# Turning the normal rows of six tiles by transposing transfers instead of TensorE, with the gates and deltas one tile later

## The chip, the cores and the metric

The kernel runs on one core of a Trainium2 chip. The metric is device time in microseconds of one execution; lower is better. An execution has five engines: TensorE (PE in the profile, its weight loads PEld), VectorE (DVE), ScalarE (ACT), GpSimd (POOL) and SyncE (SP), which here only issues transfers.

## The reference

Two residual steps on `x` of shape 2 x 1024 x 2048 (16 tiles of 128 rows):

```python
def _L0_xattn_ref(x1, x2, ...):            # fake_quant: round to 8-bit codes, and back
    return jnp.matmul(fake_quant(x1, ...), fake_quant(x2, ...))

def _L0_ffn_ref(x, A, B, Wr):              # 4 experts of rank 16, the best 2 per row
    logits = flat @ Wr.T
    gates = softmax(logits where it is one of the top 2, else -inf)
    mid = jnp.einsum('tf,erf->ter', flat, A)
    all_deltas = jnp.einsum('ter,eor->teo', mid, B) * SCALE
    return jnp.sum(gates[:, :, None] * all_deltas, axis=1)

x = x + jnp.tanh(g_xattn[0]) * _L0_xattn_ref(_layernorm(x), ctx_4096, ...)
x = x + jnp.tanh(g_ffn[0]) * _L0_ffn_ref(_layernorm(x), A, B, Wr)
```

## The kernel before, in words

Raw Bass, one program per engine, each written out in order and held together by semaphores. `ctx` is kept in SBUF as 8-bit codes in fp16 (`q2`), 16 blocks of 128 rows by 2048 columns per batch. Rows of x go through these steps, tile by tile, with five slots of `xr` (RING) in a ring:

- **codes**: `stats_x`, `var_x`, `scale_of_x` on VectorE (with `power_x` on GpSimd between), `scale_x` on ScalarE makes the byte codes, `turn_q1` on TensorE turns them into PSUM (`ps_gate`), `copy_q1T` on ScalarE brings them to `q1T`. `sum_codes` and `shift_of_row` carry a correction for the second batch.
- **product**: `main(b, n)` on TensorE, 16 matmuls for each of four column blocks n, into two banks `ps_main` in turn. `add_main(b, n)` on VectorE adds the result to `xr`; main(b, n) waits until the add two blocks before is done.
- **normal rows**: `stats_h` per block, `var_h`, `power_h` (GpSimd), `bias_h`; then `high_part` on ScalarE writes the fp16 high part `h_hi` of all 2048 columns, `normal_half` writes the fp32 value for each half, and `low_part` on GpSimd subtracts and writes the fp16 rest `h_lo`.
- **turning them**: `turn_hi(b, h)` on TensorE turns one half (8 blocks of 128x128) of `h_hi` into the PSUM bank `ps_turn[h]`, and `copy_hiT` on ScalarE brings it to `hT`; then `turn_lo` turns the low half into the same bank, and `copy_loT` (half 0 on ScalarE, half 1 on VectorE) brings it to the same `hT`, once `mid_hi` has used the high part.
- **small product**: `mid_hi` and `mid_lo` multiply the turned halves by `a_parts` (A and Wr) into `ps_mid`. `rank_gates` and `weigh` on VectorE (with `gate_exp` on ScalarE between) make the weighted middle values `gated`; `turn_gate` turns these into `ps_gate`, `split_gate` copies them to `gT_hi` and `gT_lo`, and `delta(b, n)` multiplies by B, two matmuls per block, into `ps_delta`. `add_delta` adds to `xr`, and `store` writes the tile out.

The order of all this is fixed by hand. Up to tile 8 (counting from 0) every call stands alone; from STEADY = 9 on a loop over b makes the order of each tile, and this is the part that the change rewrites. In one turn of it TensorE multiplies tile b, turns and multiplies the normal rows of tile b-1, makes the deltas of tile b-2, and turns the codes of tile b+1:

```python
for b in range(STEADY, TILES):
    main(b, 0, general, 0, 4)
    delta(b - 2, 0)
    delta(b - 2, 1)
    ...
    main(b, 2, general, 10)
    if b < LAST:
        turn_q1(b + 1, b - 1)
    mid_lo(b - 1, 0)
    mid_lo(b - 1, 1)
    main(b, 3, general, 0, 14)
    turn_gate(b - 1, min(b + 2, TILES))
    main(b, 3, general, 14)
```

After the loop comes a tail for tile 15 alone, which is not changed but for the counts of its waits. SP issues all transfers in one order of its own: in each turn the two stores of tile b-2, then, once these have landed, the two loads of tile b+3.

## Time and profile before

| | us |
|---|---|
| median of 3 runs (lowest to highest) | 359.08 (357.84 to 359.25) |
| the profiled execution's own time | 358.96 |
| its span, first to last instruction | 357.1 |
| busy in the span: TensorE, VectorE, ScalarE, GpSimd | 331.5, 280.4, 268.9, 109.4 |
| mean granted TensorE clock | 0.998 of full |

A busy share is a mean over stages with different limits. The windows view gives the busy time of each engine in a stretch; the chain of waits follows the work that ended last back from the last instruction; the timeline lists instructions in order of their start, each with its duration and what ended the idle time before it. A matmul's end is modelled, and it overlaps the next one, so its duration there (0.38 us for 512 columns) is longer than its share in the chain.

### The profile page before, as it was taken

How to read it: one execution, taken by the hardware profiler on the slowest of the kernel's cores; microseconds unless marked ns; L12 is line 12 of the kernel's file. 1: busy time of each engine (PE TensorE's matmuls, PEld its weight loads, DVE VectorE, ACT ScalarE, POOL GpSimd, SP SyncE). 2: the span in 40 equal slices, each digit the busy share in tenths (PEclk: the TensorE clock that was granted, in tenths of full speed). 3: DMA queues.
4: the chain of work that ended last, by engine and by line, in shares of the span. 5: the costliest groups of instructions: out<-in, count | busy, mean ns of one | idle time of the engine just before them, and what ended most of it. 6: DMA issues, size and time to landing. Idle time of an engine off the chain costs nothing.

```text
span 357.1 us, 6514 instructions
## 1 busy us (share of the span) xinstructions
PE 331.5 (93%) x2372; PEld 186.5 (52%) x2372; DVE 280.4 (79%) x701; ACT 268.9 (75%) x239; POOL 109.4 (31%) x123
## 2 busy tenths in 40 slices
PE   0489999999999999999999999999999999999984
PEld 0134544456665465545566565655656464656552
DVE  5798679978879778974888968779696969784785
ACT  1699799999999989898995566667858666666150
POOL 3100333245647161333432050505042240505000
PEclk9999999999999999999999999999999999999999
DMA  7999999904299759796024940423323111102023
GB/s 216 415 419 422 418 419 417 422 37 129 108 317 392 208 196 295 284 338 215 13 106 169 300 147 35 162 75 123 118 102 135 59 61 60 61 0 119 0 111 127
DMA packets 19185, 69.17 MB, mean 194 GB/s; under 512 B 2256, under 2 KB 2256, under 8 KB 19024
## 3 DMA queue, kind: packets, MB, share of 16 engines
q1 hardware_dynamic: 19152, 68.73, 51.6%
q8 instruction: 21, 0.34, 0.4%
q14 instruction: 12, 0.10, 0.1%
HBM read 51.94 MB, written 16.78 MB: 192 GB/s over the span
## 4 chain that ended last, share of the span: by engine, by line
PE 72%; DMA 11%; DVE 7%; issue 3%; ACT 3%; SPq 2%; POOL 1%; DVEq 0%; ACTq 0%; POOLq 0%
PE ps_main L741 40%; DMA xr<-in_x 6%; DMA out_x<-xr 5%; PE ps_delta L741 4%; PE ps_mid L797 4%; PE ps_turn L785 3%; PE ps_turn L778 3%; PE ps_turn L741 3%; PE ps_delta L824 3%; PE ps_delta L826 3%; PE ps_gate L741 2%; PE ps_mid L741 2%; PE ps_mid L805 2%; DVE small_tile L1236 1%; DVE xr L1292 1%
## 5 line engine op out<-in xcount | busy, mean ns | idle before, releaser
L741 PE MATMUL ps_main<-q,q1T 128*128 128x512 f16 x832 | 201.3, 379 | 1.5 <-DVE xr L1292 0.8
L741 PEld LDWEIGHTS ps_main<-q,q1T 128*128 128x128 f16 x832 | 76.8, 98 | 84.2 <-issue 8.7
L414 POOL TENSOR_TENSOR h_parts<-work,h_parts 128x512 f16<-128x512 f32 x30 | 34.2, 1160 | 53.4 <-ACT work L547 53.4
L541 ACT ACTIVATE h_parts<-xr,small_tile 128x2048 f16<-128x2048 f32 x15 | 31.4, 2092 | 24.6 <-DVE small_tile L1309 23.2
L1236 DVE BATCH_NORM_STATS2 small_tile<-xr 128x6 f32<-128x512 f32 x64 | 40.8, 682 | 7.4 <-DMA xr<-in_x 7.3
L1292 DVE SCALAR_TENSOR_TENSOR xr<-ps_main,small_tile,xr 128x512 f32<-128x512 f32 x52 | 38.6, 743 | 9.3 <-PE ps_main L741 9.3
L507 ACT ACTIVATE c_code<-q,small_tile 128x1024 uint8<-128x1024 f32 x32 | 37.8, 1236 | 9.5 <-DMA q<-in_ctx 8.3
L1297 DVE BATCH_NORM_STATS2 small_tile<-xr 128x6 f32<-128x512 f32 x64 | 43.7, 688 | 0.8
L553 ACT COPY hT<-ps_turn 128x1024 f16<-128x1024 f16 x32 | 31.4, 1006 | 13.4 <-PE ps_turn L778 13.3
L405 POOL TENSOR_TENSOR small_tile<-small_tile 128x1 f32<-128x1 f32 x16 | 8.8, 549 | 99.6 <-DVE small_tile L1305 99.6
L514 ACT ACTIVATE x_byte<-xr,small_tile 128x2048 uint8<-128x2048 f32 x16 | 33.4, 2090 | 6.6 <-DVE small_tile L1251 6.6
L414 POOL TENSOR_TENSOR h_parts<-q1T,h_parts 128x512 f16<-128x512 f32 x30 | 34.2, 1161 | 2.1 <-ACT q1T L547 2.1
L824 PE MATMUL ps_delta<-lora_bT,gT_hi 128*128 128x512 f32 x60 | 30.5, 508 | 0.2
L531 ACT ACTIVATE q1T<-ps_gate,small_tile 128x2048 f16<-128x2048 uint8 x12 | 23.5, 1961 | 2.3 <-PE ps_gate L724 2.3
L712 PE MATMUL ps_main<-ident_h 128*128 128x512 f16 x47 | 13.3, 432 | 12.5 <-issue 12.5
L400 POOL TENSOR_TENSOR small_tile<-small_tile 128x1 f32<-128x1 f32 x16 | 9.3, 584 | 49.9 <-DVE small_tile L1243 49.9
L1315 DVE COPY hT<-ps_turn 128x1024 f16<-128x1024 f16 x16 | 11.0, 689 | 17.2 <-PE ps_turn L785 17.0
L507 ACT ACTIVATE q<-q,small_tile 128x1024 uint8<-128x1024 f32 x20 | 24.3, 1236 | 0.2
L826 PE MATMUL ps_delta<-lora_bT,gT_lo 128*128 128x512 f32 x60 | 23.8, 396 | 0.0
L1366 DVE TENSOR_TENSOR xr<-ps_delta,xr 128x512 f32<-128x512 f32 x32 | 21.5, 682 | 1.0 <-PE ps_delta L826 0.8
L1223 DVE TENSOR_SCALAR q<-c_code,small_tile 128x1024 f16<-128x1024 f16 x32 | 18.9, 597 | 4.2 <-ACT c_code L507 4.0
L1369 DVE SCALAR_TENSOR_TENSOR xr<-ps_delta,small_tile,xr 128x512 f32<-128x512 f32 x30 | 21.6, 743 | 0.8 <-PE ps_delta L837 0.6
(132 smaller groups left out, 501.3 us busy)
## 6 DMA issues: line engine op xcount, KB each, us to landing
q<-in_ctx SPq DMA_DIRECT2D x52, 512.0 KB, 14.9
xr<-in_x SPq DMA_DIRECT2D x32, 512.0 KB, 6.2
out_x<-xr SPq DMA_DIRECT2D x30, 512.0 KB, 3.7
c_code<-in_ctx SPq DMA_DIRECT2D x6, 512.0 KB, 5.9
q1T<-in_ctx SPq DMA_DIRECT2D x6, 512.0 KB, 6.3
h_parts<-in_B SPq DMA_DIRECT2D x1, 1024.0 KB, 17.6
out_x<-xr SPq DMA_DIRECT2D x4, 256.0 KB, 2.2
xr<-in_A SPq DMA_DIRECT2D x1, 544.0 KB, 16.5
```

Of the source, the lines that this page charges most:

```text
L414: nc.gpsimd.tensor_tensor(h_lo[:, half(h)][:, part], work[h][:, part], h_hi[:, half(h)][:, part], ALU.subtract).then_inc(h_lo_ready, 1)
L507: nc.scalar.activation(byte, stage(i), ACT.Identity, bias=par[:, 3:4], scale=inv_s[:, 1:2]).then_inc(row_scaled, 1)
L514: nc.scalar.activation(x_byte[:, :], xr[:, b % RING, :], ACT.Identity, bias=q_scale[:, 1:2], scale=q_scale[:, 0:1]).then_inc(x_scaled, 1)
L531: nc.scalar.activation(q1T_of(b).rearrange("p (j two) m -> p j two m", two=2), as16(turn_bank(b), U8).rearrange("p (j m two) -> p j two m" ...
L541: nc.scalar.activation(h_hi[:, :], xr[:, b % RING, :], ACT.Identity, bias=h_bias[:, b % 2:b % 2 + 1], scale=h_rstd[:, b % 2:b % 2 + 1]).th ...
L553: nc.scalar.copy(hT[:, h, :, :], as16(ps_turn[h], F16).rearrange("p (k m) -> p k m", m=P)).then_inc(hiT_ready, 1)
L741: mm = pe.matmul(product_bank(b, n)[:, :], q1T_of(b)[:, k, :], q2[:, batch(b), slot(batch(b), k), cols(n)], start=(k == 0), stop=(k == KT ...
L824: pe.matmul(ps_delta[n % 2][:, :], gT_hi[:, :], lora_bT[:, cols(n)], start=True, stop=False)
L826: pe.matmul(ps_delta[n % 2][:, :], gT_lo[:, :], lora_bT[:, cols(n)], start=False, stop=True).then_inc(delta_done, 1)
L1236: nc.vector.bn_stats(x_stats[:, n, :], xr[:, b % RING, cols(n)]).then_inc(x_stats_done, 1)
L1292: nc.vector.scalar_tensor_tensor(out=x1, in0=product_bank(b, n)[:, :], scalar=gain[:, 0:1], in1=x1, op0=ALU.mult, op1=ALU.add).then_inc(x1 ...
L1297: nc.vector.bn_stats(h_stats[:, b % 2, n, :], xr[:, b % RING, cols(n)]).then_inc(h_stats_done, 1)
```

## The change

For the tiles in MOVED (8 to 13 counted from 0, which the words of the change count as 9 to 14) the eight blocks of each half are turned by a transposing transfer from SBUF to SBUF on SP's queue: `move_hi` from `h_hi` to `hT`, and `move_lo` from `h_lo` to a buffer of its own, `loT`, which lies on the fourth plane of `q1T`. The four turns on TensorE and the four copies (three on ScalarE, one on VectorE) are not made for these tiles. `mid_hi` and `mid_lo` wait for the transfers instead, `high_part` and `low_part` wait until the transfer of the tile before has read the old values, and `mid_hi` and `mid_lo` stand later among the products.

The counts of the other waits on `hi_turned`, `hiT_ready`, `lo_turned` and `loT_ready` go by `turned(b)`, the number of tiles before b that TensorE turns. The core of the diff, with the indentation cut by eight:

```diff
+MOVED = range(STEADY - 1, 14)
...
+def turned(b):
+    return len([t for t in range(b) if t not in MOVED])
+def moved(b):
+    return len([t for t in range(b) if t in MOVED])
...
+loT = q1T[:, 3, :, :].rearrange("p (h k) m -> p h k m", h=2)
...
+    def move_hi(b, h):
+        sp.wait_ge(h_hi_ready, b + 1)
+        sp.wait_ge(hi_used, 2 * (b - 1) + h + 1)
+        sp.wait_ge(lo_used, 2 * turned(b))
+        sp.dma_start_transpose(hT[:, h, :, :], h_hi[:, half(h)]).then_inc(hi_moved[h], 16)
+
+    def move_lo(b, h):
+        sp.wait_ge(h_lo_ready, 4 * b + 2 * h + 2)
+        sp.wait_ge(row_scaled, 4 * KT)
+        sp.wait_ge(lo_used, 2 * (b - 1) + h + 1)
+        sp.dma_start_transpose(loT[:, h, :, :], h_lo[:, half(h)]).then_inc(lo_moved[h], 16)
...
     for b in range(STEADY, TILES):
-        for h in range(2):
-            store(b - 2, h)
+        if b - 1 in MOVED:
+            move_hi(b - 1, 0)
+            move_hi(b - 1, 1)
+            move_lo(b - 1, 0)
+            store(b - 2, 0)
+            move_lo(b - 1, 1)
+            store(b - 2, 1)
+        else:
+            for h in range(2):
+                store(b - 2, h)
         if b + 3 < TILES:
             load_x(b + 3, 0)
             load_x(b + 3, 1)
...
         pool.wait_ge(h_hi_ready, b + 1)
-        wait(pool, lo_turned, 2 * (b - 1) + h + 1)
+        if b - 1 in MOVED:
+            pool.wait_ge(lo_moved[h], 16 * moved(b))
+        else:
...
     for b in range(STEADY, TILES):
         power_h(b - 1)
         low_part(b - 1, 0)
-        low_part(b - 1, 1)
         if b < LAST:
             power_x(b + 1)
+        low_part(b - 1, 1)
     power_h(LAST)


...
-        wait(act, hi_turned, 2 * b)
+        if b - 1 in MOVED:
+            for h in range(2):
+                act.wait_ge(hi_moved[h], 16 * moved(b))
+        else:
+            wait(act, hi_turned, 2 * turned(b))
...
     for b in range(STEADY, TILES):
+        if b > STEADY:
+            gate_exp(b - 2)
         high_part(b - 1)
         normal_half(b - 1, 0)
         normal_half(b - 1, 1)
-        copy_hiT(b - 1, 0)
-        copy_hiT(b - 1, 1)
+        if b - 1 not in MOVED:
+            copy_hiT(b - 1, 0)
+            copy_hiT(b - 1, 1)
         if b < LAST:
             scale_x(b + 1)
-        copy_loT(b - 1)
+        if b - 1 not in MOVED:
+            copy_loT(b - 1)
         if b < LAST:
             copy_q1T(b + 1)
-        gate_exp(b - 1)
-        if b < LAST:
             sum_codes(b + 1)
+        else:
+            gate_exp(b - 1)

     act.wait_ge(h_bias_ready, TILES)
-    act.wait_ge(hi_turned, 2 * LAST)
+    act.wait_ge(hi_turned, 2 * turned(LAST))
     act.wait_ge(h_lo_ready, 4 * LAST)
     for h in range(2):
         nc.scalar.activation(h_hi[:, half(h)], xr[:, LAST % RING, half(h)], ACT.Identity,
...
     def mid_lo(b, h):
-        pe.wait_ge(loT_ready[h], b + 1)
+        if b in MOVED:
+            pe.wait_ge(lo_moved[h], 16 * moved(b + 1))
+        else:
+            pe.wait_ge(loT_ready[h], turned(b) + 1)
         for k in range(HK):
             kk = h * HK + k
-            mm = pe.matmul(ps_mid[:, J:2 * J], hT[:, h, k, :], a_parts[:, kk, 0, :], start=False, stop=(kk == KT - 1))
+            mm = pe.matmul(ps_mid[:, J:2 * J], (loT if b in MOVED else hT)[:, h, k, :], a_parts[:, kk, 0, :], start=False, stop=(kk == KT - 1))
         mm.then_inc(lo_used, 1)
     def turn_gate(b, q1):
...
         turn_gate(7, 10)
         main(8, 3, general, 13, 16)
         for b in range(STEADY, TILES):
-            main(b, 0, general, 0, 4)
-            delta(b - 2, 0)
-            delta(b - 2, 1)
-            main(b, 0, general, 4)
+            main(b, 0, general)
+            if b == STEADY:
+                delta(b - 2, 0)
+                delta(b - 2, 1)
+            main(b, 1, general, 0, 6)
+            if b > STEADY:
+                turn_gate(b - 2, b + 1)
+            main(b, 1, general, 6, 12)
+            if b > STEADY:
+                delta(b - 2, 0)
+                delta(b - 2, 1)
+            main(b, 1, general, 12)
+            if b - 1 not in MOVED:
+                turn_hi(b - 1, 0)
+                turn_hi(b - 1, 1)
+            main(b, 2, general, 0, 10)
             delta(b - 2, 2)
             delta(b - 2, 3)
-            main(b, 1, general)
-            turn_hi(b - 1, 0)
-            turn_hi(b - 1, 1)
-            main(b, 2, general, 0, 10)
+            main(b, 2, general, 10, 12)
             mid_hi(b - 1, 0)
-            turn_lo(b - 1, 0)
+            if b - 1 not in MOVED:
+                turn_lo(b - 1, 0)
+            main(b, 2, general, 12)
             mid_hi(b - 1, 1)
-            turn_lo(b - 1, 1)
-            main(b, 2, general, 10)
+            if b - 1 not in MOVED:
+                turn_lo(b - 1, 1)
+            main(b, 3, general, 0, 2)
             if b < LAST:
                 turn_q1(b + 1, b - 1)
-            mid_lo(b - 1, 0)
-            mid_lo(b - 1, 1)
-            main(b, 3, general, 0, 14)
-            turn_gate(b - 1, min(b + 2, TILES))
+            main(b, 3, general, 2, 6)
+            if b - 1 not in MOVED:
+                mid_lo(b - 1, 0)
+                mid_lo(b - 1, 1)
+            main(b, 3, general, 6, 14)
+            if b - 1 in MOVED:
+                mid_lo(b - 1, 0)
+                mid_lo(b - 1, 1)
             main(b, 3, general, 14)
+            if b - 1 not in MOVED:
+                turn_gate(b - 1, TILES)
         delta(LAST - 1, 0)
         delta(LAST - 1, 1)
         pe.wait_ge(x1_ready, NB * LAST + 3)
...
     stats_h(8, 2)
     for b in range(STEADY, TILES):
-        split_gate(b - 2)
+        if b > STEADY:
+            rank_gates(b - 2)
+        else:
+            split_gate(b - 2)
         add_main(b - 1, 3)
         stats_h(b - 1, 3)
         var_h(b - 1)
-        add_delta(b - 2, 0)
+        if b > STEADY:
+            weigh(b - 2)
         bias_h(b - 1)
-        add_delta(b - 2, 1)
         if b < LAST:
             stats_x(b + 1, 0)
         add_main(b, 0)
+        if b > STEADY:
+            split_gate(b - 2)
+        else:
+            add_delta(b - 2, 0)
         shift_of_row(b)
         stats_h(b, 0)
-        add_delta(b - 2, 2)
-        add_delta(b - 2, 3)
         if b < LAST:
             stats_x(b + 1, 1)
             var_x(b + 1)
+        if b > STEADY:
+            add_delta(b - 2, 0)
+        add_delta(b - 2, 1)
         add_main(b, 1)
-        stats_h(b, 1)
         if b < LAST:
             scale_of_x(b + 1)
-        copy_loT(b - 1)
+        add_delta(b - 2, 2)
+        add_delta(b - 2, 3)
+        stats_h(b, 1)
+        if b - 1 not in MOVED:
+            copy_loT(b - 1)
         add_main(b, 2)
-        rank_gates(b - 1)
+        if b == LAST:
+            rank_gates(b - 1)
         stats_h(b, 2)
-        weigh(b - 1)
+        if b == LAST:
+            weigh(b - 1)
     split_gate(LAST - 1)
     add_main(LAST, 3)
     stats_h(LAST, 3)
```

Three places show what it moves. On TensorE, the small product of tile 13 and around it, in the time of tile 14 (L741 and L785 are the products, L797 and L844 `mid_hi`, L805 and L855 `mid_lo`; `h_parts` is `h_hi` and `h_lo`, `q1T` beside `a_parts` is `loT`). Before:

```order
L778 MATMUL ps_turn0<-ident_h,h_parts 128x128 x8
L778 MATMUL ps_turn1<-ident_h,h_parts 128x128 x8
L741 MATMUL ps_main0<-q2,q1T 128x512 x10
L797 MATMUL ps_mid<-a_parts,hT 128x136 x8
L785 MATMUL ps_turn0<-ident_h,h_parts 128x128 x8
L797 MATMUL ps_mid<-a_parts,hT 128x136 x8
L785 MATMUL ps_turn1<-ident_h,h_parts 128x128 x8
L741 MATMUL ps_main0<-q2,q1T 128x512 x6
L724 MATMUL ps_gate<-ident_h,x_byte 128x128 x8
L805 MATMUL ps_mid<-a_parts,hT 128x68 x16
L741 MATMUL ps_main1<-q2,q1T 128x512 x14
L816 MATMUL ps_gate<-ident_f,gated 128x128
```

Now:

```order
L785 MATMUL ps_main0<-q2,q1T 128x512 x2
L844 MATMUL ps_mid<-a_parts,hT 128x136 x8
L785 MATMUL ps_main0<-q2,q1T 128x512 x4
L844 MATMUL ps_mid<-a_parts,hT 128x136 x8
L785 MATMUL ps_main1<-q2,q1T 128x512 x2
L768 MATMUL ps_gate<-ident_h,x_byte 128x128 x8
L785 MATMUL ps_main1<-q2,q1T 128x512 x12
L855 MATMUL ps_mid<-a_parts,q1T 128x68 x16
L785 MATMUL ps_main1<-q2,q1T 128x512 x2
```

The four turns are gone; `mid_hi` of half 0 stands 12 products into block 2, and `mid_lo` two products ahead of the end of block 3, where it stood ahead of block 3.

On VectorE, the start of tile 15's time. Before (L1357 and L1359 are `split_gate`, L1292 `add_main`, L1369 `add_delta`):

```order
L1357 CAST gT_hi<-ps_gate 128x128
L1359 TENSOR_TENSOR gT_lo<-ps_gate,gT_hi 128x128
L1292 SCALAR_TENSOR_TENSOR xr<-ps_main1,small_tile,xr 128x512
L1297 BN_STATS small_tile<-xr 128x6
L1302 BN_AGGR small_tile<-small_tile 128x2
L1305 TENSOR_SCALAR small_tile<-small_tile 128x1
L1369 SCALAR_TENSOR_TENSOR xr<-ps_delta0,small_tile,xr 128x512
L1309 TENSOR_SCALAR small_tile<-small_tile 128x1
L1369 SCALAR_TENSOR_TENSOR xr<-ps_delta1,small_tile,xr 128x512
```

Now (the ranking of tile 13 stands ahead of the first row; L1360 is `add_main`, L1409 to L1417 are `weigh`, L1377 is `bias_h`, L1425 and L1427 are `split_gate`):

```order
L1360 SCALAR_TENSOR_TENSOR xr<-ps_main1,small_tile,xr 128x512
L1365 BN_STATS small_tile<-xr 128x6
L1370 BN_AGGR small_tile<-small_tile 128x2
L1373 TENSOR_SCALAR small_tile<-small_tile 128x1
L1409 SCALAR_TENSOR_TENSOR ps_mid<-ps_mid,small_tile 128x64
L1413 TENSOR_REDUCE small_tile<-ps_mid 128x1
L1415 RECIPROCAL small_tile<-small_tile 128x1
L1417 SCALAR_TENSOR_TENSOR gated<-mids,small_tile,ps_mid 128x128
L1377 TENSOR_SCALAR small_tile<-small_tile 128x1
L1360 SCALAR_TENSOR_TENSOR xr<-ps_main0,small_tile,xr 128x512
L1425 CAST gT_hi<-ps_gate 128x128
L1427 TENSOR_TENSOR gT_lo<-ps_gate,gT_hi 128x128
```

Ranking and weighing of tile b-2, at the end of tile b-1's time before, now stand around `var_h` of tile b-1, and `split_gate` behind the first block of tile b.

On SP, the stores and loads from tile 10's loads on. Before:

```order
L269 DMA xr<-in_x 128x1024 x4
L290 DMA out_x<-xr 128x1024 x2
L269 DMA xr<-in_x 128x1024 x2
L290 DMA out_x<-xr 128x1024 x2
L269 DMA xr<-in_x 128x1024 x2
```

Now:

```order
L282 DMA xr<-in_x 128x1024 x4
L309 DMA_TRANSPOSE hT<-h_parts 128x8x128 x2
L315 DMA_TRANSPOSE q1T<-h_parts 128x8x128
L303 DMA out_x<-xr 128x1024
L315 DMA_TRANSPOSE q1T<-h_parts 128x8x128
L303 DMA out_x<-xr 128x1024
L282 DMA xr<-in_x 128x1024 x2
```

Four transposing transfers stand in each turn, two ahead of the stores' place and two among them.

## Rows read from the trace of the kernel before

**Rows 1.** The page's part 1, busy us, share of the span and instructions.
```profile
PE 331.5 (93%) x2372; PEld 186.5 (52%) x2372; DVE 280.4 (79%) x701; ACT 268.9 (75%) x239; POOL 109.4 (31%) x123
```

**Rows 2.** Windows: length, then busy us of each engine, clock, DMA share, GB/s.
```profile
core 0: us, PE busy (x) PEld busy (x) DVE busy (x) ACT busy (x) POOL busy (x), PEclk, DMA share, GB/s
200.80:339.00 138.20, 137.78 (x1008) 78.96 (x1007) 106.61 (x280) 89.32 (x85) 38.44 (x41) 1.00 0.25 93
240.25:260.00 19.75, 19.71 (x147) 11.34 (x145) 15.74 (x42) 13.62 (x13) 5.56 (x6) 1.00 0.31 109
```

**Rows 3.** Chain of waits, time of tile 11: start us, us, what.
```profile
238.04 1.29 PE ps_main L741 x6
239.34 0.23 PE ps_delta L824
...
247.26 0.89 PE ps_turn L778 x16
...
250.31 0.47 PE ps_mid L797 x8
250.78 0.45 PE ps_turn L785 x8
...
253.89 0.50 PE ps_mid L805 x16
...
257.45 0.33 PE ps_gate L816
257.78 1.29 PE ps_main L741 x6
```

**Rows 4.** Timeline, tile 11's time: start, us, engine, line, operation, tiles, idle before.
```profile
242.14 1.28 DVE L1236 BATCH_NORM_STATS2 small_tile<-xr 128x6 f32<-128x512 f32 x2
...
243.33 0.73 DVE L1292 SCALAR_TENSOR_TENSOR xr<-ps_main,small_tile,xr 128x512 f32<-128x512 f32 x1
...
244.90 2.28 POOL L414 TENSOR_TENSOR h_parts<-work,h_parts 128x512 f16<-128x512 f32 x2 [3.59 <-ACT work L547]
...
254.43 0.31 DVE L1322 TENSOR_REDUCE ps_mid<-ps_mid 128x68 f32<-128x136 f32 x1 [0.19 <-PE ps_mid L805]
...
255.80 0.68 DVE L1297 BATCH_NORM_STATS2 small_tile<-xr 128x6 f32<-128x512 f32 x1
...
256.40 0.22 DVE L1341 SCALAR_TENSOR_TENSOR ps_mid<-ps_mid,small_tile 128x64 f32<-128x64 f32 x1
...
257.04 0.35 DVE L1349 SCALAR_TENSOR_TENSOR gated<-mids,small_tile,ps_mid 128x128 f32<-128x128 f32 x1
...
258.35 0.74 DVE L1292 SCALAR_TENSOR_TENSOR xr<-ps_main,small_tile,xr 128x512 f32<-128x512 f32 x1
...
260.34 0.75 DVE L1369 SCALAR_TENSOR_TENSOR xr<-ps_delta,small_tile,xr 128x512 f32<-128x512 f32 x1
...
261.33 2.09 ACT L541 ACTIVATE h_parts<-xr,small_tile 128x2048 f16<-128x2048 f32 x1 [3.03 <-DVE small_tile L1309]
```

**Rows 5.** Timeline, the end of tile 15's products.
```profile
332.30 0.66 PE L805 MATMUL ps_mid<-a_parts,hT 128*128 128x68 f16 x16
...
333.17 0.30 DVE L1322 TENSOR_REDUCE ps_mid<-ps_mid 128x68 f32<-128x136 f32 x1
...
336.55 0.29 DVE L1357 CAST gT_hi<-ps_gate 128x128 fp32r<-128x128 f32 x1 [0.42 <-PE ps_gate L816]
...
336.89 0.50 PE L824 MATMUL ps_delta<-lora_bT,gT_hi 128*128 128x512 f32 x1
337.08 0.74 DVE L1292 SCALAR_TENSOR_TENSOR xr<-ps_main,small_tile,xr 128x512 f32<-128x512 f32 x1
```

**Rows 6.** The page's parts 3 and 6: the queue, and stores to landing.
```profile
q1 hardware_dynamic: 19152, 68.73, 51.6%
...
out_x<-xr SPq DMA_DIRECT2D x30, 512.0 KB, 3.7
...
out_x<-xr SPq DMA_DIRECT2D x4, 256.0 KB, 2.2
```

19 lines of the change are left out of this document (12 added, 7 removed).

## The prediction

> **What bounds the kernel now.** I read the page's busy shares first: TensorE is busy for 93% of the span, VectorE for 79%, ScalarE for 75% [rows 1]. A mean over stages says little, so the windows come next. In the steady part, 200.8 to 339 us, TensorE is busy 137.78 of 138.20 us at full granted clock, and in the window of one tile (240.25 to 260.00) it is busy 19.71 of 19.75 us, against 15.74 for VectorE and 13.62 for ScalarE [rows 2]. There TensorE alone sets the time, and what leaves its stream is gained until some other chain is late. The chain of waits, third, shows what one tile's 19.74 us (238.04 to 257.78) is made of: products at 1.29 us for six, 0.215 each; 0.89 us for the 16 transposes of the high part; 0.45 us for each 8 of the low part, twice; 0.47 us for each half of the high product; 0.50 us for the low product; 0.33 us for the gate's turn; 0.23 us for each of 8 delta matmuls [rows 3].
>
> **The change part by part.** *Transposes off TensorE.* Each of six tiles (9 to 14 in the title's count, indices 8 to 13 in the code, turned in the time of tiles 9 to 14) loses 0.89 + 2 x 0.45 = 1.79 us of transposes [rows 3]. All of it lies on the path: 6 x 1.79 = **-10.74 us**. One transpose costs 0.056 us there, since they run in a stream. The Trainium skill, VectorE: DVE Perf Modes, section The three transpose paths, has 390 ns for a 128x128 turn on TensorE; by an estimate from that page the 192 would be worth 75 us. The trace disagrees with 56 ns, and the measurement decides. ScalarE loses three copies a tile and VectorE one; neither bounds, so they count as nothing. If TensorE stopped bounding they would matter, and VectorE, at 15.74 us less one copy against a new period of about 18.0, has only some 3 us of slack.
>
> *Gates and deltas moved.* rank_gates, weigh and split_gate of tile b-2 now run in tile b, ahead of or between the steps that make tile b-1's normal rows. The question is whether the new order keeps pace. I lay it out from the start of rank_gates(b-2) as 0, with the intervals of the old order [rows 4]. Ranking takes 1.37 us (254.43 to 255.80). add_main, stats_h and var_h take 1.99 (258.35 to 260.34), so weigh starts at 3.36; it reaches its last operation after 0.64 and ends at 4.35. bias_h follows at about 4.3, h_hi's activation 0.25 later, and it ends after 2.09 us at 6.6. stats_x starts at 4.4, add_main(b, 0) 1.19 later at 5.6, the cast to gT_hi about 0.65 after that (0.73 us less the overlap), and it ends at 6.53. On TensorE, the low product that released rank_gates ended 0.04 us before 0. Then come 24 products (5.18), the gate's turn (0.33; its operand has been there since 4.4) and six products (1.29), so the first delta matmul should end at about 7.0. In the last tile, where a delta found its weights not yet loaded, it ended 0.55 us after the cast did (336.84 to 337.39) [rows 5]: here 7.08. The two weights together make me put **+0.2 us** on each of five tiles, **+1.0 us** in all, with 0 and 0.4 a tile as ends. The same delay covers turn_q1, whose codes come at 14.35 by this reckoning, just when TensorE wants them. delta(b-2, 2) and (b-2, 3) want their banks at 10.7 and 11.2 and VectorE frees them at 10.3 and 10.9: no wait, but little room.
>
> *The last tile.* There tile 14 is still turned by TensorE, but mid_lo(14) stands six products later than before: 6 x 0.215 = **+1.30 us**. Everything after it hangs on VectorE: rank_gates started at 333.17 and the last add_main at 337.08, 3.91 us later, with the same operations between them as in the new order [rows 5]. So TensorE's products, which now end 2.16 us after mid_lo, no longer cover that chain, and the engine idles for about a microsecond ahead of the gate's turn. What comes back is that rank_gates, which waited 0.21 us past mid_lo's end (332.96) for VectorE [rows 5], will wait 0.04: **-0.17 us**.
>
> *The four transfers a tile.* SP issues each one when its source half is ready. The high halves come at 6.65 and are wanted at 12.1 and 13.4 (12 and 16 products into the third column block). GpSimd starts the first low half at 7.85 and needs 2.28 us for it [rows 4], so it goes out at 10.2 and is wanted at 17.4; the second, after power_x, goes out at 13.0 and is wanted at 17.6. The queue also carries the stores, and the second load_x of an iteration waits for them; those loads are out by about 17 and SP is next wanted at 24.6, so SP blocks nothing. No row shows a transposing transfer. From below, a store of the same 256 KB landed in 2.2 us, of which 0.7 is the bytes at the queue's mean rate while busy (68.73 MB in 51.6% of 357.1 us, 0.373 MB/us) and 1.5 is fixed [rows 6]. From above: the queue's 19152 packets took 51.6% of 16 engines' 357.1 us, 154 ns each [rows 6]. If each 256-byte run of a row costs as much as such a packet, a half is 1024 runs, 64 an engine, 9.9 us, and 11.4 with the fixed part. Call the queue time of a half D, between 0.7 and 9.9. Nothing is late while 8.15 + 2D stays under 13.4 and 8.15 + 4D + 1.3 (a store between) under 17.6, which is D up to 2.0. I take D = 1.5, near the lower end: it is what the stores pay for 256 KB more (3.7 against 2.2) [rows 6], the nearest row by bytes, and double the mean rate's price. So the transfers cost nothing, hidden behind the 5 to 7 us of products ahead of each use.
>
> Sum: -10.74 + 1.0 + 1.30 - 0.17 = -8.6 us. The profiled execution took 358.96 us (span 357.1); that gives 350.3. It stands 0.12 us under the median of 359.08, so no further shift.
>
> **The rivals.** *Transposing transfers are slow (slower than before).* If the price goes by short runs, the queue runs without a pause from 6.65 on and mid_lo waits for the fourth half: each tile is late by 9.45 + 4D - 17.6. The 8.6 us are used up at 1.4 us a tile, D = 2.4; past that the kernel is slower. At D = 4, the geometric middle between my value and the upper end, a tile is 7.85 us late, the total 358.96 - 8.6 + 6 x 7.85 = 397 us; at 9.9 it would be about 540. For it: four small-run transfers a tile in series, and the one bound that rows give from above. Against it: the queue is busy for 25% of the steady part [rows 2], and the bytes are few. I give it 18%. The same section of the Trainium skill speaks against this change: it has 1309 ns for a 128x128 turn by transfer and advises TensorE where a PSUM destination will do; eight blocks in series would be 10.5 us a half by an estimate from it, this rival at its upper end. No row here shows it.
>
> *A new VectorE chain takes most of it.* The margins above are 0.1 to 0.4 us and rest on some 25 intervals. If the chain to gT_hi, or to add_delta, runs 0.5 to 1 us longer, TensorE waits that much in each of five tiles: 352.8 to 355.3. Together with transfers a little late (D 2.0 to 2.3) I give it 14%. For it: VectorE has waits of its own between nearly all of these small operations. Against it: the intervals come from the same operations in the same form.
>
> *No gain to be seen*, where D is close to 2.4, or the tail loses several us more than I have: 358 or 359 us, 8%. That the transfers are not made, or made late because SP stands at another wait, I hold to be out: they stand in SP's order, and no wait ahead of them ends after 17 us of the previous tile's time.
>
> **How the numbers follow.** Forecast as above 60%, its own range 348.3 to 352.5 (0 to 0.4 us of wait a tile, and 1 us for the tail). To take in the second case and the third the range goes up to 360.9; 18% lie above, nearly nothing below. A measurement of this kernel can tell some 0.5%, 1.8 us, from no change: faster by more 0.74, within it 0.08, slower by more 0.18.
>
> **What the new profile would show.** Right: a tile's period of 18.0 to 18.3 us in the chain of waits; 192 fewer transposes on TensorE; no wait for hT or q1T ahead of the products of a_parts; transfers landing 3 to 5 us after issue; about 0.2 us at the delta behind the cast to gT_hi; 1 us idle before the last turn of a gate. Wrong: a TensorE wait released by a DMA in each tile (the slow transfers), or by gT_hi, x_byte or out_ready for over 0.4 us a tile (the VectorE chain); or a granted clock under 1 in the tail from the added idle time.

## The result, and the profile after

| | before | after |
|---|---|---|
| median of 4 runs each, us | 358.92 (357.84 to 359.25) | 349.29 (349.14 to 350.64) |
| ratio, 95% interval | | 0.9744 (0.9722 to 0.9765) |
| profiled execution, us (span) | 358.96 (357.1) | 350.64 (348.9) |
| period of a steady tile, us | 19.76 | 18.12 |
| from the seventh index's gate cast to the last one, us | 152.13 | 143.10 |

The changed kernel is 2.6% faster; 350.3 us had been predicted. Medians here and in the table of experiments are over executions in the fast state; the two slower ones, 393.37 us in experiment 2 and 352.95 us in experiment 4, are left out. The last row of the table needs a word. Executions of one kernel reach the steady part at different times: the cast to gT_hi of tile index 7, the last one that no experiment here touches, stands at 198.36 us in the profile before and at 199.14 after, and over all runs below between 196.9 and 199.6. From there on a tile's period repeats to 0.02 us in most kernels. So small effects are read from that cast to the last cast of the program. These are VectorE's timeline rows of the kernel before:

```profile
198.36 0.29 DVE L1357 CAST gT_hi<-ps_gate 128x128 fp32r<-128x128 f32 x1 [0.30 <-PE ps_gate L816]
...
350.49 0.29 DVE L1357 CAST gT_hi<-ps_gate 128x128 fp32r<-128x128 f32 x1 [0.42 <-PE ps_gate L816]
```

and the same two of the kernel after:

```profile
199.14 0.29 DVE L1425 CAST gT_hi<-ps_gate 128x128 fp32r<-128x128 f32 x1 [0.29 <-PE ps_gate L866]
...
342.24 0.29 DVE L1425 CAST gT_hi<-ps_gate 128x128 fp32r<-128x128 f32 x1 [0.42 <-PE ps_gate L866]
```

By this measure the change brought 152.13 - 143.10 = 9.03 us. The page of the kernel after, its parts 1 and 3:

```profile
PE 321.4 (92%) x2180; PEld 175.4 (50%) x2180; DVE 276.0 (79%) x695; ACT 252.2 (72%) x221; POOL 109.5 (31%) x123
...
DMA packets 44528, 75.45 MB, mean 216 GB/s; under 512 B 27600, under 2 KB 27600, under 8 KB 44368
...
q1 hardware_dynamic: 44496, 75.02, 63.3%
```

TensorE has the 192 matmul instructions less that the order of work had promised [rows 1]. The queue carries 25344 packets more than before [rows 6], 1056 for each of the 24 transposing transfers, and is busy for 0.633 x 348.9 - 0.516 x 357.1 = 36.6 us more, 1.52 us a half. The next answer is the stretch of one tile, from one first delta to the next, in the windows view:

```profile
core 0: us, PE busy (x) PEld busy (x) DVE busy (x) ACT busy (x) POOL busy (x), PEclk, DMA share, GB/s
...
241.67:259.80 18.13, 18.07 (x113) 9.44 (x114) 14.70 (x41) 10.80 (x12) 5.58 (x6) 1.00 0.68 175
```

TensorE still looks busy for 18.07 of 18.13 us, at full granted clock, as before [rows 2]. The share of busy time hides what the chain of waits shows:

```profile
240.77 0.65 DVE xr L1360
241.42 0.21 DVE gT_hi L1425
241.67 0.50 PE ps_delta L874
...
252.66 0.51 PE ps_mid L855 x16
253.20 0.32 DVE ps_mid L1390
...
258.90 0.65 DVE xr L1360
259.55 0.21 DVE gT_hi L1425
259.80 0.50 PE ps_delta L874
```

Before, the chain stayed on TensorE for the whole tile [rows 3]. Now the turns (L778 and L785 of the kernel before) are gone, and in each tile the chain leaves TensorE at the low product (253.20), runs for 6.6 us through VectorE (ranks, the fourth add_main, statistics, weigh, add_main(b, 0)) to gT_hi and comes back with the first delta. That is a closed loop at the pace of the tile. The waits of the stretch from 200 to 320 us name it, and the room that VectorE has left elsewhere:

```profile
DVE ps_mid L1390 <- PE ps_mid L855: 16.2, 6, 3.0
...
PEld ps_delta L874 <- DVE gT_hi L1425: 2.7, 5, 0.6
PEld ps_gate L768 <- ACT x_byte L550: 1.5, 5, 0.3
```

TensorE's weight load waits for gT_hi in five tiles, while VectorE stood idle 2.7 us ahead of ranking, for the low product. The weight load of the codes' turn waits too, 0.3 us a tile, but the turn itself starts no later behind its products than in experiment 1 below (0.43 us from the first of its two products to it, 249.03 to 249.46). No wait is released by a transfer. The four transfers of this tile in SP's timeline:

```profile
241.73 2.59 SPq L309 DMA_TRANSPOSE hT<-h_parts  x2
245.22 1.23 SPq L315 DMA_TRANSPOSE q1T<-h_parts  x1
246.51 1.42 SPq L303 DMA_DIRECT2D out_x<-xr  x1
248.03 1.60 SPq L315 DMA_TRANSPOSE q1T<-h_parts  x1
249.68 0.57 SPq L303 DMA_DIRECT2D out_x<-xr  x1
252.93 0.81 SPq L282 DMA_DIRECT2D xr<-in_x  x2
```

With the start of ranking at 235.07 (253.20 less a period), the reckoning of the prediction has them at 241.72, 245.27 and 248.07. The time to landing is in the two lines' own answers, first L309, then L315:

```profile
DMA to landing us min/median/max: 2.7/2.7/2.8
DMA to landing us min/median/max: 2.7/2.7/4.4
```

The medians hide something. The second low half, the last of the four, landed after 2.7 us in the first two moved tiles, but after 3.6, 4.4, 4.4 and 4.2 us in the other four. TensorE wants it when the second half of the low product starts, 0.25 us into that product. In the tile of 266.12 us it landed at 270.52 and was wanted at 270.88: the room was 0.36 us (landings are given to 0.1 us), and 1.1 us in the tile shown.

At the end of tile 15, TensorE's timeline shows the idle time that the late low product of tile index 14 leaves [rows 5 for before]:

```profile
324.20 0.66 PE L855 MATMUL ps_mid<-a_parts,hT 128*128 128x68 f16 x16
...
327.92 0.33 PE L866 MATMUL ps_gate<-ident_f,gated 128*128 128x128 f32 x1 [0.90 <-DVE gated L1417]
328.63 0.50 PE L874 MATMUL ps_delta<-lora_bT,gT_hi 128*128 128x512 f32 x1 [0.38 <-DVE gT_hi L1425]
```

### The profile page after: what moved, and what is told of

It is laid out like the page before. It is cut to its first block, busy times and chain, and to the rows that moved or that the text cites. A ratio compares the mean times of both kernels' runs of the same rounds, so it can differ in the third digit from the quotient of the medians.

```text
span 348.9 us, 6112 instructions
## 1 busy us (share of the span) xinstructions
PE 321.4 (92%) x2180; PEld 175.4 (50%) x2180; DVE 276.0 (79%) x695; ACT 252.2 (72%) x221; POOL 109.5 (31%) x123
## 4 chain that ended last, share of the span: by engine, by line
PE 62%; DVE 14%; DMA 12%; issue 4%; ACT 3%; SPq 3%; POOL 1%; DVEq 0%; ACTq 0%; POOLq 0%
PE ps_main L785 32%; DMA out_x<-xr 5%; DMA xr<-in_x 4%; PE ps_delta L785 4%; PE ps_mid L844 4%; DMA q<-in_ctx 4%; PE ps_delta L874 3%; PE ps_turn L785 3%; PE ps_delta L876 3%; DVE xr L1360 3%; DVE small_tile L1304 2%; PE ps_mid L785 2%; PE ps_gate L785 2%; PE ps_mid L855 2%; PE ps_turn L829 2%
## 5 line engine op out<-in xcount | busy, mean ns | idle before, releaser
L785 PE MATMUL ps_main<-q,q1T 128*128 128x512 f16 x832 | 201.9, 379 | 2.8 <-DVE xr L1360 2.0
L785 PEld LDWEIGHTS ps_main<-q,q1T 128*128 128x128 f16 x832 | 76.1, 98 | 84.4 <-issue 8.6
L1360 DVE SCALAR_TENSOR_TENSOR xr<-ps_main,small_tile,xr 128x512 f32<-128x512 f32 x52 | 38.5, 741 | 3.4 <-PE ps_main L785 3.4
L1291 DVE TENSOR_SCALAR q<-c_code,small_tile 128x1024 f16<-128x1024 f16 x32 | 20.5, 647 | 3.7 <-ACT c_code L543 3.5
L844 PEld LDWEIGHTS ps_mid<-a_parts,hT 128*128 128x128 f16 x256 | 17.3, 98 | 7.1 <-issue 1.0
L456 POOL MEMSET q<- 128x1024 f32 x16 | 15.1, 955 | 18.1 <-ACT q L543 9.3
```

The source lines that it names most:

```text
L785: mm = pe.matmul(product_bank(b, n)[:, :], q1T_of(b)[:, k, :], q2[:, batch(b), slot(batch(b), k), cols(n)], start=(k == 0), stop=(k == KT ...
L844: mm = pe.matmul(ps_mid[:, 0:2 * J], hT[:, h, k, :], a_parts[:, kk, :, :].rearrange("p c j -> p (c j)"), start=(kk == 0), stop=False)
L1360: nc.vector.scalar_tensor_tensor(out=x1, in0=product_bank(b, n)[:, :], scalar=gain[:, 0:1], in1=x1, op0=ALU.mult, op1=ALU.add).then_inc(x1 ...
```

## The experiments

Eleven kernels were run. All but the seventh start from the kernel after; tile numbers in them are the program's indices, so the six moved tiles are 8 to 13 and the last is 15. "Cast to cast" is the measure of the section above; differences between kernels are by it unless a clock time is named. Each ratio is to executions of the kernel before that were taken beside it, with medians of 358.73 us for experiments 1 to 4, 359.24 for 5 to 8 and 359.63 for 9 to 11, so it is not the quotient of two rows of the table.

| kernel | median, us | ratio to before, 95% | cast to cast, us | period, us |
|---|---|---|---|---|
| before | 358.92 | | 152.13 | 19.76 |
| after | 349.29 | 0.9744 (0.9722 to 0.9765) | 143.10 | 18.12 |
| 1 order only | 358.69 | 1.0001 (0.9987 to 1.0015) | 151.80 | 19.50 |
| 2 three tiles | 354.04 | 0.9856 (0.9827 to 0.9886) | 147.65 | 18.12, then 19.5 |
| 3 tile 14 too | 348.92 | 0.9719 (0.9696 to 0.9742) | 141.82 | 18.12 |
| 4 tile 14, deltas later | 347.22 | 0.9700 (0.9673 to 0.9728) | 141.61 | 18.08 |
| 5 low product sooner | 348.48 | 0.9703 (0.9682 to 0.9724) | 141.25 | 17.70 to 17.87 |
| 6 much sooner | 348.30 | 0.9705 (0.9664 to 0.9746) | 141.21 | 17.72 to 17.84 |
| 7 before, gate later | 359.89 | 1.0019 (1.0002 to 1.0036) | 152.47 | 19.87 |
| 8 last tile as before | 349.19 | 0.9736 (0.9704 to 0.9769) | 141.96 | 18.12 |
| 9 transfers only | 355.99 | 0.9902 (0.9875 to 0.9928) | 149.09 | 19.23 |
| 10 low halves twice | 355.98 | 0.9905 (0.9877 to 0.9933) | 149.52 | 18.9 to 19.7 |
| 11 tile 14 and sooner | 346.39 | 0.9622 (0.9599 to 0.9645) | 139.39 | 17.70 to 17.79 |

### 1. The order alone

```diff
-MOVED = range(STEADY - 1, 14)
+MOVED = range(STEADY - 1, STEADY - 1)
...
-                    if b - 1 not in MOVED:
+                    if b == LAST:
                         turn_gate(b - 1, TILES)
```

> The changed kernel's order of work with no tile moved: TensorE turns both parts of every tile, 192 transposes more than in the changed kernel, while gates, deltas and low products stay a tile later than before. My theory (the gain is the 192 transposes, and the new order costs about 1.3 us at the end): 359 to 361 us, a period of 19.7 to 20.0 us per tile in the steady part, ratio to the kernel before 1.000 to 1.006. Rival (the gain comes from the new order, which takes waits off TensorE): 350 to 355 us. A second rival (the new order costs more than the sum had, and the transposes brought more than 10.7 us): above 361 us.

Measured: 358.69 us, ratio 1.0001, no difference by the clock; 151.80 us cast to cast, 0.33 less than before. So on top of the new order the transfers bring 151.80 - 143.10 = 8.70 us; what they bring without it is experiment 9. But the period was not what I had expected. TensorE's timeline of this kernel:

```profile
242.51 0.27 PE L866 MATMUL ps_gate<-ident_f,gated 128*128 128x128 f32 x1
...
243.72 0.58 PE L874 MATMUL ps_delta<-lora_bT,gT_hi 128*128 128x512 f32 x1
...
262.01 0.27 PE L866 MATMUL ps_gate<-ident_f,gated 128*128 128x128 f32 x1
```

Gate to gate is 19.50 us, 0.26 under the kernel before. This order therefore has a floor for the changed kernel: 19.51 - 1.79 = 17.72 us, not the 17.97 that one gets from the period before. And from the gate's turn to the first delta, with the same six products between, this kernel takes 243.72 - 242.51 = 1.21 us. The kernel after takes 1.62:

```profile
258.18 0.27 PE L866 MATMUL ps_gate<-ident_f,gated 128*128 128x128 f32 x1
258.29 1.46 PE L785 MATMUL ps_main<-q,q1T 128*128 128x512 f16 x6
259.80 0.50 PE L874 MATMUL ps_delta<-lora_bT,gT_hi 128*128 128x512 f32 x1
```

The wait for gT_hi thus costs 0.41 us a tile, twice what the sum had, and the new order gave back 0.25 a tile that the sum did not have.

### 2. Three tiles instead of six

```diff
-MOVED = range(STEADY - 1, 14)
+MOVED = range(STEADY - 1, 11)
...
```

The condition of the last turn_gate is changed as in experiment 1.

> Only tiles 8 to 10 of the program's count (three of six) are turned by transfers; tiles 11 to 13 go through TensorE in the new order. My theory (each moved tile gains by itself, 1.79 us of transposes less about 0.2 us of new wait): 349.3 + 3 x 1.6 = 354.1 us, between 353.6 and 355.0. Rival (the gain is one step, had once from the order): within 1 us of 349.3 or of 359. In the trace: tiles 8 to 10 at a period of 18.1 us, tiles 11 to 13 at 19.7 to 20.0.

Measured: 354.04 us, 147.65 cast to cast. The first three moved tiles bring 151.80 - 147.65 = 4.15 us, the next three 4.55. Both come out of the two numbers of experiment 1: three tiles' transposes at 1.79 us, less 0.41 us for each wait at gT_hi. Three such waits are in this kernel's timeline (1.62 us from gate to first delta, then 1.21), and two more in the kernel after, since tile 15 has none: 5.37 - 1.23 = 4.14 and 5.37 - 0.82 = 4.55. The gain is had tile by tile; the rival of one step falls.

### 3. Tile 14 by transfer as well

```diff
-MOVED = range(STEADY - 1, 14)
+MOVED = range(STEADY - 1, 15)
...
-                    if b - 1 not in MOVED:
+                    if b == LAST:
                         mid_lo(b - 1, 0)
                         mid_lo(b - 1, 1)
...
```

The waits of the tail on the turns of tile 14 become waits on its landings. mid_lo(14) stays behind six products of the fourth block, where the kernel after has it; the expectation has it four products later, which is not what the edit does.

> Tile 14 of the program's count is turned by transfers as well, so that only the last tile's normal rows go through TensorE. 32 more transposes leave TensorE (1.79 us), and mid_lo(14) comes another four products later, behind the landing of the second low half. My theory (TensorE sets the period, transfers are hidden): 349.3 - 1.8 + 0.2 = 347.7 us, between 347.3 and 348.3. Rival 1 (the tail is bound by VectorE's ranks and add_mains after mid_lo, so that a later mid_lo costs as much as the transposes give): 349.3 us or more, up to 350.5. Rival 2 (transfers collide with the last loads and stores): a wait of TensorE on a landing in tile 15.

Measured: 348.92 us by the clock, hardly a difference; 141.82 cast to cast, 1.28 less than after, where 1.6 was expected. Rival 2 is there in a small way: this is the first transfer that TensorE waits for, since mid_lo stands early in this tile. TensorE's timeline:

```profile
322.69 0.41 PE L856 MATMUL ps_mid<-a_parts,q1T 128*128 128x68 f16 x8
323.45 0.42 PE L856 MATMUL ps_mid<-a_parts,q1T 128*128 128x68 f16 x8 [0.34 <-DMA q1T<-h_parts]
...
326.93 0.33 PE L867 MATMUL ps_gate<-ident_f,gated 128*128 128x128 f32 x1 [0.90 <-DVE gated L1418]
```

The second half of the low product starts 0.76 us behind the first instead of 0.25, so the landing costs 0.51 us, and 1.79 - 0.51 is the 1.28 measured. The 0.90 us ahead of the gate's turn is as it was: VectorE's chain behind the low product still sets the end.

### 4. Tile 14, with deltas and codes two products later

The edit of experiment 3, and besides:

```diff
-                    main(b, 1, general, 6, 12)
+                    main(b, 1, general, 6, 14)
                     if b > STEADY:
                         delta(b - 2, 0)
                         delta(b - 2, 1)
-                    main(b, 1, general, 12)
+                    main(b, 1, general, 14)
...
-                    main(b, 3, general, 0, 2)
+                    main(b, 3, general, 0, 4)
                     if b < LAST:
                         turn_q1(b + 1, b - 1)
-                    main(b, 3, general, 2, 6)
+                    main(b, 3, general, 4, 6)
```

> As the run with tile 14 too, and besides in every steady tile both halves of the delta come two products later in TensorE's order (behind 14 products instead of 12), and the turn of the next tile's codes two products later as well. My theory (VectorE's rank chain ends 0.16 us per tile after TensorE wants the first delta, and the codes come in step with it, so both have to move): 347.7 - 6 x 0.15 = 346.8 us, between 346.4 and 347.3, period 17.97 to 18.0. Rival (the wait merely moves on, because VectorE's next add_main or rank comes later by as much, a closed loop): within 0.3 us of the run with tile 14 too.

Measured: a period of 18.08 us and 141.61 cast to cast, 0.21 less than the run before it. The rival was right. The wait for gT_hi is gone (1.65 us from gate to first delta, with eight products between), but the next one stands behind it, at the second pair of deltas. TensorE's timeline here, from the first of the twelve products ahead of that pair:

```profile
240.86 1.47 PE L786 MATMUL ps_main<-q,q1T 128*128 128x512 f16 x6
...
243.56 0.47 PE L875 MATMUL ps_delta<-lora_bT,gT_hi 128*128 128x512 f32 x1
...
244.22 0.47 PE L875 MATMUL ps_delta<-lora_bT,gT_hi 128*128 128x512 f32 x1
```

and in the kernel after, with fourteen products ahead of it:

```profile
242.80 1.47 PE L785 MATMUL ps_main<-q,q1T 128*128 128x512 f16 x6
...
245.65 0.58 PE L874 MATMUL ps_delta<-lora_bT,gT_hi 128*128 128x512 f32 x1
```

The pair comes 2.70 us behind the first product here and 2.85 there. Two products less are 0.43 us less, so it starts 0.28 us late; it then takes 1.21 us instead of 1.13. Together that is 0.36 us, all that the period lies above 17.72. The view of waits names no releaser for it (eight waits of the weight load, 3.1 us in four tiles), but the two add_delta that free the banks are in VectorE's timeline from 242.67 to 244.08, and the second delta starts 0.14 us behind the end of the second:

```profile
242.67 1.41 DVE L1438 SCALAR_TENSOR_TENSOR xr<-ps_delta,small_tile,xr 128x512 f32<-128x512 f32 x2
```

Moving the consumer back doesn't help in a closed loop; the start of VectorE's chain has to come sooner. By the clock this kernel looks 1.7 us better than the third. In the two profiled executions, 347.19 and 349.62 us, the difference is 2.43 us, and 2.22 of it stands at the cast of tile index 7 (197.20 against 199.42 us), ahead of anything that the two do differently. That is the spread of the start, not the edit.

### 5. The low product two products sooner

```diff
-                    main(b, 3, general, 6, 14)
+                    main(b, 3, general, 6, 12)
                     if b - 1 in MOVED:
                         mid_lo(b - 1, 0)
                         mid_lo(b - 1, 1)
-                    main(b, 3, general, 14)
+                    main(b, 3, general, 12)
```

> The changed kernel with mid_lo(b-1) two products sooner (behind 12 products of the fourth block instead of 14) in the five steady tiles. VectorE stood idle 2.7 us a tile for this product, and its chain from there to gT_hi set TensorE's wait of 0.41 us a tile (18.12 us against 19.51 - 1.79 = 17.72 by the run of the order alone). My theory now: the chain starts 0.43 us sooner, the wait is gone, a period of 17.70 to 17.80 us, 5 x 0.4 = 2.0 us less from the first moved tile's cast to the last cast than the changed kernel's 143.10: 141.1; by the clock some 347.3 us, with the 1 us by which executions of one kernel differ before the steady part. Rival 1 (the wait is set by something else than VectorE's start, its own length or the ring of buffers): 18.08 to 18.12. Rival 2 (the second low half lands too late for the sooner product): a TensorE wait released by the transfer into q1T, and a period between the two.

Measured: 141.25 us cast to cast (141.1 expected), ratio 0.9703. From gate to first delta TensorE now takes 1.22 us, as in the first experiment:

```profile
256.12 0.27 PE L866 MATMUL ps_gate<-ident_f,gated 128*128 128x128 f32 x1
...
257.34 0.58 PE L874 MATMUL ps_delta<-lora_bT,gT_hi 128*128 128x512 f32 x1
```

The period is 17.70 us in three of five tiles, 17.78 and 17.87 in two. This shows both the floor of 17.72 and the cause of the 0.41 us: the loop started late by two products, while VectorE stood idle ahead of it.

The two longer tiles are the transfer's, as far as the times tell. In them the low product, 0.66 us long in the other tiles, lasts 0.73 and 0.83 us:

```profile
249.94 0.73 PE L855 MATMUL ps_mid<-a_parts,q1T 128*128 128x68 f16 x16
```

The other stands at 285.43. There the second low half was handed out at 281.33 and landed 4.5 us later, at 285.83, where its product wanted it at 285.68; in the tile shown it landed at 250.21 and was wanted at 250.19. In the tiles of 17.70 us it landed in time. The view of waits lists nothing as short as 0.07 or 0.17 us, so this rival 2, small, is read from the times and not named by the profile.

### 6. Four products sooner

The same edit with 10 in the place of 12.

> mid_lo(b-1) four products sooner (behind 10 products). In the changed kernel the second low half is handed out at 248.03 us and takes up to 4.0 us to land, 252.0; this order wants it at 251.6 less 0.4 for the shorter period. My theory (transfers were hidden with 0.5 to 1 us to spare and no more): TensorE waits 0.2 to 0.9 us a tile for the transfer, so that the period is 17.9 to 18.6 us, worse than with two products sooner. Rival (the margin is large, transfers are never late): no wait on a transfer, a period of 17.72.

Measured: a period of 17.72 us in three tiles, 17.74 and 17.84 in the last two, and no wait on a transfer in the view of waits; the rival was right about the period. But the margin is small. The second low half landed after 2.7 us in the first two tiles and after 3.7 to 4.4 us in the last four, about as long as I had taken it for. What I had wrong is when it is handed out: the sooner low product starts VectorE's next chain sooner too, so that the half goes out at 246.38 us, 1.93 us ahead of the codes' turn, where the kernel after has 1.43. The second half of the low product wants it at 250.74, 4.36 us later. In the last tile it landed at 303.96 and was wanted at 303.92, and that low product lasts 0.78 us instead of 0.66: the 0.12 us of the 17.84. Four products are not better than two, since TensorE is at its floor with either, and later than here the transfer must not land.

### 7. The kernel before, with the gate's turn later

```diff
-                    main(b, 0, general, 0, 4)
+                    main(b, 0, general, 0, 6 if b > STEADY else 4)
                     delta(b - 2, 0)
                     delta(b - 2, 1)
-                    main(b, 0, general, 4)
+                    main(b, 0, general, 6 if b > STEADY else 4)
...
-                    main(b, 3, general, 0, 14)
+                    main(b, 3, general)
                     turn_gate(b - 1, min(b + 2, TILES))
-                    main(b, 3, general, 14)
```

> The kernel before, with the turn of the gate two products later (behind the whole fourth block) and, so as to keep the distance, the first two deltas two products later too, in the steady part. My theory (the kernel before lost 0.25 us a tile because TensorE stood at the gate's turn until VectorE had written gated; the sum took that loss for work): a period of 19.50 to 19.55 us against 19.76, 6 x 0.22 = 1.3 us less, 357.4 us, ratio 0.996. Rival (the 0.25 us that the order alone brought comes from the other moves): a period of 19.74 to 19.78, no change.

Measured: 359.89 us, ratio 1.0019 (1.0002 to 1.0036), a period of 19.87 us in the profile, longer by 0.11 us a tile; a ratio of 1.0019 is at the edge of what the medians tell. Neither theory had that. The gate's turn now takes its plain 0.11 us, but the low product waits instead, for ScalarE's copy of the turned low half, in TensorE's timeline:

```profile
254.53 0.67 PE L805 MATMUL ps_mid<-a_parts,hT 128*128 128x68 f16 x16 [0.21 <-ACT hT L558]
```

In the kernel before, it was the weight load of the gate's turn that waited, in its waits of the same stretch:

```profile
PEld ps_gate L816 <- DVE gated L1349: 1.6, 3, 0.5
```

So the 0.25 us of the kernel before was also the loss of a loop, and two products more at one place move it. Which of the moves in the new order breaks that loop (the copies, the statistics of x, the deltas) is not told apart by these runs; that the whole of them does is shown by the first.

### 8. The last tile in its old order

```diff
...
+                    if b == LAST:
+                        mid_hi(b - 1, 0)
+                        turn_lo(b - 1, 0)
+                        mid_hi(b - 1, 1)
+                        turn_lo(b - 1, 1)
+                        main(b, 2, general, 10)
+                        mid_lo(b - 1, 0)
+                        mid_lo(b - 1, 1)
+                        main(b, 3, general, 0, 14)
...
```

The other tiles keep the order of the kernel after.

> The changed kernel with mid_hi(14), turn_lo(14) and mid_lo(14) of the last tile back at their places in the kernel before, six products sooner for mid_lo. My theory (the end of tile 15 is bound by VectorE's chain of 3.9 us behind mid_lo(14), during which TensorE idles for 1.28 us): the last rank and all behind it come up to 1.30 us sooner, less what the copy of the low part to hT, also on VectorE and ScalarE, still needs: 0.5 to 1.3 us less from the rank of tile 13 to the last cast, some 348.4 us. Rival (TensorE's products or high_part(14) hold the end): within 0.2 us of the changed kernel.

Measured: 141.96 us cast to cast, 1.14 less than after. TensorE's idle time ahead of the gate's turn is gone:

```profile
321.61 0.66 PE L855 MATMUL ps_mid<-a_parts,hT 128*128 128x68 f16 x16
322.11 3.61 PE L785 MATMUL ps_main<-q,q1T 128*128 128x512 f16 x16
325.56 0.27 PE L866 MATMUL ps_gate<-ident_f,gated 128*128 128x128 f32 x1
```

The median, 349.19 us, is still that of the kernel after: 1.1 us is within what the start varies by, over six runs.

### 9. The transfers without the new order

The loops of TensorE, VectorE, ScalarE and GpSimd over the steady tiles are those of the kernel before, with the turns and copies of moved tiles left out; SP's loop is that of the kernel after.

> The same six tiles turned by transfers, with the order of work of the kernel before on TensorE, VectorE, ScalarE and GpSimd (gates and deltas not moved, mid_lo at the start of the fourth block). My theory (the transfers need the later low product that the moved gates make room for): GpSimd writes the second low half at about 249.6 us of tile 11's time in the kernel before, a transfer takes up to 4.0 us from there, 253.6, and mid_lo, no longer behind 1.79 us of transposes, wants it at 251.9: TensorE waits 1 to 1.7 us a tile on the landing, a period of 19.0 to 19.7 us, 353 to 358 us. Rival 1 (the new order was not needed): a period of 17.97 (19.76 less 1.79), 348.2 to 349 us. Rival 2 (VectorE's rank, behind the late low product, pushes the gate's turn and the next tile's deltas as well, so that the loss adds up): over 20 us, slower than before.

Measured: 355.99 us, ratio 0.9902, a period of 19.23 us. The size was as expected, the cause was not. No transfer is late; TensorE waits for the codes of the next tile, by its timeline:

```profile
250.51 0.62 PE L767 MATMUL ps_gate<-ident_h,x_byte 128*128 128x128 f16 x8 [1.09 <-ACT x_byte L550]
```

The six products ahead of it start at 247.97 and are worth 1.29 us, so the turn comes 1.25 us late, which is nearly all that the period lies above 19.76 - 1.79 = 17.97 us. The weight load of the gate's turn waits 0.5 us a tile as well, as it does in the kernel before. In the old order VectorE comes to the second part of the statistics of x (244.00 us) only after the deltas of tile b-2, and ScalarE starts the codes at 248.36: too late for a TensorE that is 1.79 us ahead. That it is the deltas' place and not another of the moves is read from the order, not tested. So of the 9.03 us that the change brought, 3.04 come with the transfers in the old order (152.13 - 149.09), 0.33 with the new order alone, and the other 5.7 only when both are there.

### 10. Each low half transferred twice

```diff
+                wait(sp, lo_moved[h], 32 * moved(b))
+                sp.dma_start_transpose(spare[:, h, :, :], h_lo[:, half(h)]).then_inc(lo_moved[h], 16)
                 sp.dma_start_transpose(loT[:, h, :, :], h_lo[:, half(h)]).then_inc(lo_moved[h], 16)
...
-                    pe.wait_ge(lo_moved[h], 16 * moved(b + 1))
+                    pe.wait_ge(lo_moved[h], 32 * moved(b + 1))
```

`spare` lies on `c_code`; GpSimd's wait on the transfers counts by 32 as well.

> The changed kernel with each low half transferred twice, first into a spare tile, then into its place, so two more transfers a tile on the same queue. One issue occupied SP for 1.24 us, a landing took 2.7 to 4.4 us. My theory (the low halves are hidden with about 1 us to spare; the queue's time of a half is 1.5 us): the second low half is handed out 2.2 us later, at 250.2, and lands near 253.7 where TensorE wants it at 252.75: 0.5 to 1.5 us of wait a tile, 352 to 358 us. Rival 1 (transfers have several us of room): a period of 18.12, no change. Rival 2 (transfers collide with stores and loads once the queue is fuller): over 2 us a tile, more than 361 us.

Measured: 355.98 us, 149.52 cast to cast, 6.4 more than after, 1.07 us a moved tile. The waits of four tiles' time, 240 to 313 us:

```profile
PEld ps_mid L858 <- DMA q1T<-h_parts: 5.3, 4, 1.8
PE ps_mid L858 <- DMA q1T<-h_parts: 4.8, 4, 1.6
```

TensorE is idle 1.2 us a tile for the landing. The mechanism of the slow-transfer rival is real, then: two more halves in the series are enough to set it off. It did not decide because a half takes 1.5 us of the queue and not 2.4.

### 11. Both edits that gained

```diff
-MOVED = range(STEADY - 1, 14)
+MOVED = range(STEADY - 1, 15)
...
-                    main(b, 3, general, 6, 14)
-                    if b - 1 in MOVED:
+                    main(b, 3, general, 6, 12)
+                    if b < LAST:
                         mid_lo(b - 1, 0)
                         mid_lo(b - 1, 1)
-                    main(b, 3, general, 14)
+                    main(b, 3, general, 12)
...
```

The rest is that of experiment 3.

> Tile 14 of the program's count turned by transfers too, and mid_lo(b-1) two products sooner in the steady tiles: what the two runs that gained most did, together. From the first moved tile's cast to the last cast the changed kernel took 143.10 us; tile 14 brought 1.28 and the sooner low product 1.85. My theory (the two losses lie in different tiles and add): 140.0 us, between 139.7 and 140.4, by the clock about 346.2 us. Rival (the end is bound by VectorE's chain whatever comes ahead of it, so that the one takes back the other's gain): 141.0 to 141.3.

Measured: 346.39 us, ratio 0.9622 (0.9599 to 0.9645), the best of all; the whole interval lies under that of the kernel after. Its casts on VectorE:

```profile
199.57 0.29 DVE L1426 CAST gT_hi<-ps_gate 128x128 fp32r<-128x128 f32 x1 [0.30 <-PE ps_gate L867]
...
338.96 0.29 DVE L1426 CAST gT_hi<-ps_gate 128x128 fp32r<-128x128 f32 x1 [0.42 <-PE ps_gate L867]
```

The period is 17.71 us but for one of 17.79, and 139.39 cast to cast is 3.71 less than after, where 3.13 was expected: the gains add, and 0.58 us more. Of that, 0.42 is the landing in tile 15. In experiment 3 both halves of the low product took 1.02 us there (322.69 to the next product at 323.71), here 0.60 (320.84 to 321.44), of which 0.50 is work: the second low half took 3.2 us to land in both, but the sooner low product of the tile before let it go out 0.43 us sooner against TensorE (2.88 us ahead of the product instead of 2.45). The other 0.17 us is that experiment 5 had two longer tiles and this kernel one.

## Why the prediction was right

The forecast was 350.3 us, 8.6 under the profiled execution before; the medians differ by 9.6 us and the two profiles by 9.03 us cast to cast. Point by point:

- **Transposes off TensorE, -10.74 us.** Right, on the condition of the new order (in the old one the same transfers bring 3.04, experiment 9), with the chain on TensorE as the reason: without the delta's wait a tile is at 17.72 us, 1.79 under the 19.51 of the same order with the turns (experiments 1, 5 and 6). A transpose in a stream is worth 0.056 us, as the rows before had it. By the estimate from the Trainium skill's VectorE: DVE Perf Modes, The three transpose paths (390 ns each on TensorE), 192 of them would have been 75 us; the trace disagrees with it, with 10.74.
- **The wait behind gT_hi, +1.0 us.** The mechanism and the place were right, the size was not: 0.41 us a tile in five tiles, 2.05. VectorE's side came out: counted from the start of ranking, the cast ended at 6.55 us (6.53 forecast) and the first delta at 7.1 (7.08). The step that failed is TensorE's side, where that delta should have ended at 7.0 without a wait. It counted the gate's turn at 0.33 us and took the whole 19.74 us for work. Without its wait the turn takes 0.11 (experiment 1: 242.51, and the next product at 242.62), so TensorE was there 0.2 us sooner than the sum had it.
- **A term that was missing, -1.5 us.** The kernel before lost 0.25 us a tile at the gate's turn, which stood behind gated, and the view of busy time showed that as TensorE at work. The new order takes it away, 6 x 0.25. Nothing in the prediction had this; it covers the error of the point above, and that they nearly cancel is luck. The sum in terms as measured is -10.74 + 2.05 - 1.5 + 1.14 = -9.05, against -9.03.
- **The last tile, +1.30 - 0.17 us.** Right: the old order of that tile brings 1.14 (experiment 8), and what the order alone has in steady tiles, 1.5, less its 0.33 in all, leaves 1.17. The idle microsecond ahead of the gate's turn was 0.90 us, and the rank started 0.04 us behind the low product, as forecast (324.86 and 324.90).
- **Transfers hidden, D = 1.5.** Right: 1.52 us of the queue's time a half, handed out within 0.05 us of where the reckoning had them, and TensorE waited for none. The row of equal bytes was the better guide than the row of packets (154 ns each would have made it 9.9). Landing after 2.7 us was quicker than the 3 to 5 forecast in the high halves and most first low halves, but not in the last half of the later tiles, at 3.6 to 4.4. "Hidden" held with as little as 0.36 us to spare; experiments 5 and 6 use that up in single tiles. The Trainium skill has 1309 ns a block by transfer (same page and section; by an estimate 10.5 us a half), and its advice to stay on TensorE stands in that page's section Rules for kernel authors, not where the prediction puts it. Neither is borne out here: a half of eight blocks landed in 2.7 us at the median, 4.4 at most.
- **No wait at the codes, and little room at delta(b-2, 2).** Right; experiment 4 shows how little: two products later for the first deltas, and the second pair waits for its banks.

Of the rivals, the slow transfers needed two more halves a tile to come true (experiment 10). The rival of the VectorE chain had 0.5 to 1 us more of wait a tile; it was 0.21 more, and from TensorE's side, with the chain as long as reckoned. But 0.41 us stands just past the prediction's own sign of that rival, over 0.4 us a tile at gT_hi: that term was at the very end of its range, and the total didn't show it.

So the forecast of the whole was nearer than its parts: two of its terms were off by 1.05 and 1.5 us, in opposite directions. The mechanism (transposes off a bounding TensorE, transfers hidden, a small wait behind gT_hi, a late last tile) was right; the closeness of the number owes something to luck.
